# A four-layer graph network on one core: a third buffer for the radial weights, and one landing wait per block of gathers

## The reference

```python
# layer one: tensor product with per-edge weights from a small net
w  = silu(edge_attr @ w1 + b1) @ w2 + b2          # [E, 1024], "radial weights"
x0, x1 = x[src][:, :16], x[src][:, 16:].reshape(-1, 16, 3)
out0 = alpha * (einsum('eu,e,euw->ew', x0, sh0, w00) + einsum('eui,ei,euw->ew', x1, sh1, w11) / sqrt(3))
out1 = alpha * (einsum('eu,ei,euw->ewi', x0, sh1, w01) + einsum('eui,e,euw->ewi', x1, sh0, w10)) / sqrt(3)
...
# layer two: relations as sums of 8 bases; per-edge coefficients w_comp[edge_type]
# z[node, basis, :] = sum over its edges of coef[e, basis] * x[src[e]]
# layer three: graph convolution, a sum over the edges of scaled rows h[src[e]]
```

## Time and profile before

| | |
|---|---|
| median of 3 runs | 23,192.35 us |
| lowest and highest | 23,182.5 and 23,208.56 us |
| the profiled execution | 23,174.65 us |
| its span in the profile | 23,172.8 us |
| mean granted TensorE clock | 0.627 of full |

### The profile page before, as it was taken

One profiled execution on the slowest core, in us unless ns is written; L12 is line 12 of the kernel. 1 busy time (PEld: TensorE's weight loads), 2 busy tenths in 40 slices (PEclk: granted clock), 3 DMA queues, 4 the chain that ended last, 5 costly groups with the idle time before them and its releaser, 6 DMA issues. The chain is left out here.

```text
span 23172.8 us, 208220 instructions
## 1 busy us (share of the span) xinstructions
PE 10208.4 (44%) x47565; PEld 6761.2 (29%) x47566; DVE 15518.0 (67%) x25810; ACT 2702.6 (12%) x6634; POOL 12776.2 (55%) x12678
## 2 busy tenths in 40 slices
PE   0033335655555555555666632222234434344333
PEld 0033332222222222222222332222233333233333
DVE  8744447998888888887666521111477777677777
ACT  0011110000000000000000000000122332223322
POOL 0188886666565656644666426665355554455553
PEclk9999996555555555557888755555555555555555
DMA  4033331111111111111111101111422222222222
GB/s 176 21 69 69 70 69 28 24 24 24 23 22 23 22 24 21 24 22 22 24 24 24 17 13 21 21 21 20 59 61 61 56 58 51 58 63 60 57 59 47
DMA packets 1151509, 957.47 MB, mean 41 GB/s; under 512 B 803963, under 2 KB 920315, under 8 KB 1150739
## 3 DMA queue, kind: packets, MB, share of 16 engines
q0 software_dynamic: 419904, 437.84, 11.0%
q1 hardware_dynamic: 730960, 512.22, 8.6%
HBM read 734.68 MB, written 210.63 MB: 41 GB/s over the span
## 5 line engine op out<-in xcount | busy, mean ns | idle before, releaser
L1458 POOL DMA_INDIRECT tail<-ball,h_idx x3328 | 3445.4, 1035 | 3295.5 <-issue 1379.1
L737 PE MATMUL p_rad<-w_stack,hid_t 99*128 99x512 bf16 (+1 forms) x6656 | 3073.8, 619 | 2355.2 <-DVEq L827 1082.5
L1494 PE MATMUL h_sum<-head,h_hot 128*128 128x64 f32 x6656 | 1446.7, 417 | 3475.0 <-ACT head L1539 2117.5
L809 DVE TENSOR_REDUCE red<-prod 128x96 f32<-128x1536 f32 x1664 | 2900.2, 1743 | 3.5
L1494 PEld LDWEIGHTS h_sum<-head,h_hot 128*128 128x128 f32 x6656 | 1414.0, 327 | 3500.3 <-issue 3500.3
L1101 POOL DMA_INDIRECT l_xg<-h_tab,l_idx x1664 | 1573.9, 946 | 1462.7 <-issue 957.6
L338 POOL DMA_INDIRECT rec_a<-rec,slot x1600 | 1988.9, 1243 | 517.0 <-issue 501.4
L693 POOL DMA_INDIRECT rec_b<-l_rcb x1600 | 1929.8, 1206 | 570.9 <-issue 514.6
L932 POOL DMA_INDIRECT l_xg<-x_tab,l_idx x1664 | 1574.2, 946 | 1154.2 <-issue 834.1
L948 PE MATMUL l_sum<-outer,l_hot 128*128 128x512 f32 x3328 | 1684.6, 670 | 971.1 <-DVEq L993 899.5
L737 PEld LDWEIGHTS p_rad<-w_stack,hid_t 99*128 99x128 bf16 (+1 forms) x6656 | 773.3, 132 | 4300.7 <-issue 4298.8
(11 more groups left out here) (368 smaller groups left out, 18411.8 us busy)
## 6 DMA issues: line engine op xcount, KB each, us to landing
hot_t<-rows_l SPq DMA_DIRECT2D x208, 512.0 KB
rec_a<-fill SPq DMA_DIRECT2D x128, 728.0 KB, 19.6
l_rec<-rec_a SPq DMA_DIRECT2D x104, 896.0 KB, 4.8
rhot_t<-rows_r SPq DMA_DIRECT2D x208, 384.0 KB
tail<-ball,h_idx POOLq DMA_INDIRECT x3328
t<-in_type SPq DMA_DIRECT2D x100, 500.0 KB
l_xg<-in_x,l_idx POOLq DMA_INDIRECT x1664
l_xg<-x_tab,l_idx POOLq DMA_INDIRECT x1664
```

The source lines that it names most:

```text
L737: ins = pe.matmul(p_rad[j % 2][:, h * 512:(h + 1) * 512], hid_t[j // 4 % 2][0:K3 + 3 * (1 - i), j % 4, i, :], w_stack[i][0:K3 + 3 * (1 - i ...
L809: ch.step(dve.tensor_reduce(red[:, j, :], prod[j % 3][:, :, :], AX, ALU.add))
L1458: pool.indirect_dma_start(tg[q][:, j, :], None, table[:, :], bass.IndirectOffsetOnAxis(ap=idx[q][:, j:j + 1], axis=0)).then_inc(gathered[q ...
L1494: ins = pe.matmul(p_sum[u % 2][:, j % BT // 2, :], hot[j // HP8 % 2][:, j % HP8, :], hg[:, j, 0:D], start=(j % 2 == 0), stop=(j % 2 == 1))
```

## The change

In layer one the radial weights get a third buffer of two PSUM banks. PE takes tile j into buffer j % 3, makes three tiles of the next block before the sums of this one, and its waits for `tile_done` are renumbered: the first tile of a block waits for the last of the block before. In layers two and three POOL waits for landings once per block, after the sixteenth gather, and the index copies go from DVE to ACT. In layer two ACT makes them for block b+2 when block b-2 is used up, ahead of the coefficient copy of block b on its queue; in layer three for block b+4 when block b is summed.

```diff
@@ product_phase
-        p_rad = [ps(f"p_rad{q}", [P, COLS]) for q in range(2)]
+        p_rad = [ps(f"p_rad{q}", [P, COLS]) for q in range(3)]
...
             def tile(b, j):
-                hold(pe, turn, tile_done, b * BT + (j + 1))
+                hold(pe, turn, tile_done, b * BT + (3 if j == 0 else j if j < 3 else j + 1))
...
-                        ins = pe.matmul(p_rad[j % 2][:, h * 512:(h + 1) * 512], hid_t[j // 4 % 2][0:K3 + 3 * (1 - i), j % 4, i, :],
+                        ins = pe.matmul(p_rad[j % 3][:, h * 512:(h + 1) * 512], hid_t[j // 4 % 2][0:K3 + 3 * (1 - i), j % 4, i, :],
...
                 tile(b, 1)
+                tile(b, 2)
 
             def body(b, q, it, left):
-                for j in range(2, BT):
+                for j in range(3, BT):
...
-            dve.sem_inc(tile_done, SEED)
+            dve.sem_inc(tile_done, 3)
...
-                w = p_rad[j % 2][:, :].rearrange("p (a w u) -> p a w u", a=4, u=MUL)
+                w = p_rad[j % 3][:, :].rearrange("p (a w u) -> p a w u", a=4, u=MUL)
@@ relation_phase
-            with act.Fori(0, NB // 4) as it:
+            def indices(u, b):
+                act.activation(idx[u][:, :], g["src_a"][:, bass.ds(b * BT, BT)], ACT.Copy).then_inc(idx_ready, 1)
+
+            def quad(it, last):
                 for u in range(4):
                     b = it * 4 + u
+                    hold(act, turn, coef_used, b + 1)
+                    if not last or u < 2:
+                        indices((u + 2) % 4, b + 2)
                     hold(act, turn, coef_in[u], it * 32 + 32)
-                    hold(act, turn, coef_used, b + 1)
                     act.activation(p_coef[u % 2][:, 0:BT * NBAS].rearrange("p (t n) -> p t n", n=NBAS), coef[u][:, :, :], ACT.Copy).then_inc(coef_ready, 1)
+
+            for u in range(2):
+                indices(u, u)
+            with act.Fori(0, NB // 4 - 1) as it:
+                quad(it, False)
+            quad(NB // 4 - 1, True)
...
-                        if j % 8 == 7:
-                            hold(pool, turn, gathered[u], it * (16 * BT) + 16 * (j + 1))
+                    hold(pool, turn, gathered[u], it * (16 * BT) + 16 * BT)
...
-            for u in range(4):
-                dve.tensor_copy(idx[u][:, :], g["src_a"][:, u * BT:(u + 1) * BT]).then_inc(idx_ready, 1)
...
-                if left == 2:
-                    dve.tensor_copy(idx[u][:, :], g["src_a"][:, bass.ds((b + 4) * BT, BT)]).then_inc(idx_ready, 1)
@@ spread_phase: the same two edits to the gathers and to DVE, and on ACT
+            for u in range(4):
+                act.activation(idx[u][:, :], g["src_a"][:, u * BT:(u + 1) * BT], ACT.Copy).then_inc(idx_ready, 1)
+            with act.Fori(0, NB // 4 - 1) as it:
+                for u in range(4):
+                    b = it * 4 + u
+                    hold(act, turn, sum_done, b + 1)
+                    act.activation(idx[u][:, :], g["src_a"][:, bass.ds((b + 4) * BT, BT)], ACT.Copy).then_inc(idx_ready, 1)
```

## The result

The kernel before took 23,200.46 us (four runs beside the changed one, 23,182.5 to 23,209.55), the changed one 22,838.07 us (22,804.19 to 22,855.39). The ratio is 0.9843, 95% interval [0.9826, 0.986]: 362 us faster. The forecast was 22,290 us in a range up to 22,680; the time lies 158 us above the range. The sign and layer one were right, layer two went the other way.

What follows compares the result with a forecast made beforehand. DVE was taken to bound layer one, POOL's gathers and landing waits layers two and three. Savings of 385 + 260 + 257 = 902 us from 23,192 gave 22,290 us, range 22,190 to 22,680.

Steps and rivals of the forecast that it cites:

- Layer one, 385 us: Saving claimed for layer one from the third radial buffer: 153 + 312 - 80 us, with bounds of 153 and 465.
- third-tile term: Layer one: the third buffer removes DVE's stall at each block's third tile, 1.5 us x 102 blocks = 153 us.
- term for the seventh tile: Layer one: of 312 us of DVE stall at the seventh tile, about 80 us remain with PE one tile further ahead.
- late completions: Layer one: during a long gather stream, the semaphore telling DVE of a finished tile arrives late, about 3.9 us a block.
- The landing wait, 2.50 and 2.47 us a block: Layers two and three: replacing one landing wait per block by a plain gap saves 260 and 257 us.
- The page's fit for one transfer: Layers two and three: alternative estimate, 0.83 us per landing wait, 172 us saved in both; set aside for the trace.
- It stays 1.4 us below the new round: Layer two: DVE's own round of 21.05 us stays under the new 22.44 us, so the saving is whole.
- The rival of late completions: Layer two: late completions appear there, a 4 us hold per block eats the 260 us; time 22,550 us, chance 0.25.
- The slower rival: Layer two: holds of 10.2 to 12 us per block make the whole change lose, up to 23,380 us; chance 0.05.
- Layer three "has 18 us of cover and would not care": Layer three: PE waits 18 us of each 25 for gathers, so late completions would not reduce the 257 us.
- Index copies at 0: Layers two and three: moving 104 index copies per layer to ACT costs nothing; uncovered it would be 31 us.
- Thirteen early blocks without the stall: Layer one, 4,000 to 4,800 us: same gather streams, no late completions seen; argument against their appearing in layer two.

Runs made afterwards that it cites:

- a1: The changed kernel unaltered, run again beside the kernel before on another chip of the first kind: 22,640.46 us, ratio 0.987.
- e2: The kernel before with only the change to layer two, on a chip of the first kind: 23,154.7 us, ratio 1.0106.
- e1: The kernel before with only the third radial buffer of layer one, on a chip of the second kind: 22,369.22 us, ratio 0.9957.
- i1: The changed kernel unaltered, on a chip of the second kind: 21,858.33 us, ratio 0.9732.
- f2: The changed kernel with a 1.45 us POOL memset after the eighth gather in layers two and three, second kind of chip: 22,156.27 us, ratio 0.986.
- e4: The changed kernel with the landing wait per eight gathers put back in layer two, second kind of chip: 22,116.44 us, ratio 0.984.
- f3: The changed kernel with a 0.45 us POOL memset after the eighth gather in layer two, second kind of chip: 21,952.28 us, ratio 0.9765.
- g4: The kernel before with a 1.45 us POOL memset after the eighth gather in layer one, first kind of chip: 22,925.06 us, ratio 0.9985.
- e3: The kernel before with only the change to layer three, on a chip of the second kind: 22,221.84 us, ratio 0.9889.

## Why the prediction was right or wrong, step by step

**Layer one, 385 us: 388 measured.** The third-tile term, 153 us, was 152.7 in idle time. The term for the seventh tile, 312 - 80, was too small: nothing of the stall was left at DVE ("remote" 279.1 us before, 2.2 after), so idle time fell by 457. What I had not counted brought the sum back: the message and one-hot operations, 86 us longer, the message's beside POOL's features. (457 - 86 = 371; products and reductions are another 16 us shorter in sum.) The total agrees because two misses cancel, and by luck of the chip: on the chip of a1 and e2, also of the first kind, layer one goes from 6,860 to 6,589, 271 us. On the second kind the stall is absent, and of the 153 us the stage gains 107 and 112 (e1, i1) and only 91, 58 and 49 (f2, e4, f3). The longer messages take a part of the rest; why these runs differ stays open.

**The late completions, read in layer one.** "While a long stream of gathers is in flight, the semaphore that tells DVE of a finished tile arrives late": the tie to the stream is shown by g4, which added a pause to it and nothing else. The reading missed that beside a stream PE itself can slow down: in layers two and three of the result, and already in the fourth layer before, single passes stand apart.

**The landing wait, 2.50 and 2.47 us a block: right as a price.** On the second kind layer three gains 257 us (257 forecast) and layer two 2,619 - 2,368 = 251 (260 forecast). The page's fit for one transfer (the Trainium skill, DMA: Bandwidth & Descriptors, anatomy of one DMA on the SWDGE path), with its 172 us for both layers, is ruled out as the price of this wait by these 508 us. For the transfer itself the trace agrees with it: in layer two before, the last packet ends 2.12 us after the start of its gather (median of 198). POOL goes on only 1.5 us after that, and it is this which the estimate lacked.

**The step that failed** is "It stays 1.4 us below the new round. [...] So both savings are whole." It took DVE's round of 21.05 us in layer two as a property of its instructions. On the first kind of chip it depends on POOL's stream: the round became 2,875/104 = 27.6 us, DVE the bound, and the saving of 260 us a loss of 258. Against i1's 2,368 us the crawl costs 507 us, 4.9 us a block.

**The rival of late completions** (0.25) had the disturbance and its place right and named its signs. Its size was taken from layer one, one hold of 4 us per block, which would just eat the gain; DVE meets PE eight times a block there, and lost 21.05 to 27.6, 6.6 us. The slower rival had supposed 10 to 12. Truth lay between two sizes of one mechanism, and so the time came out above the range: 22,290 + 260 + 258 = 22,808, with layer three's 82 us 22,890, against 22,838 (the fourth layer, 17 us shorter in the profile, and the spread of the runs lie in the rest).

**Layer three "has 18 us of cover and would not care"** was wrong by 82 us (257 forecast, 175 measured): the crawl turns 7 us of sums into up to 32 of waiting (14563.95 above), more than the cover, and then POOL waits for its indices.

**Index copies at 0** held: i1 shows no wait on them, and where POOL waits for them it is for DVE's `coef_used` ahead of the copy.

**Thirteen early blocks without the stall** The earlier trace rows were taken as evidence against the rival, and the trace of the kernel before says otherwise. The earlier trace rows asked for DVE's waits only. In the same 800 us ACT waits under "remote" in five cases (138.0 us), and on the second kind (e3) in none. One of them, behind the last of eight transposes:

```profile
4037.06 0.31 PE L729 MATMUL l_turn<-l_ident_b,l_rec 128*96 128x128 bf16 x1
...
4042.83 1.02 ACT L713 ACTIVATE hid_t<-l_turn 96x1024 bf16<-96x1024 bf16 x1 [29.23 <-remote]
```

The copy starts 5.5 us after the transposes are modelled to end; the next one, with no gather in flight, starts 0.3 us behind its own (4047.24). So the late completions were there from the start and fell on ACT, which had idle time to spare. The one argument against the rival was a question put to one engine.

What stays open: by what path a stream of gathers slows PE, why a landing wait after eight of them is enough in two layers and not in the fourth, and why it happens on three of six chips and the result's, and not on the other three. Granted clock (0.50 in layer three in both kinds; 0.81 and 0.85 in layer two), the cadence of the gathers (1.25 us in both) and the bytes moved (957.96 and 957.94 MB) don't tell the kinds apart.

## What to carry to other kernels

A wait that looks like pure loss may also be the pause that another engine lives on. Before a landing wait is taken out, look in the trace for any place where the stream already runs that long, and ask for the waits of every engine there, not only of the one that bounds the stage: an engine with idle time can be the one that shows the disturbance. A stall found in one stage gives no size for another: once per block was too little here (4 us), once for each of eight meetings with PE would have been far too much (32 us), and 6.6 us were measured. If a stall has no releaser in the profile, run the same kernel on another chip before building a term on it: here 312 us of one sum existed on one kind of chip only. And where the wait is to go, try a short pause of known length in its place: 1.45 us after the eighth gather gave back 354 and 361 us on two chips of one kind, and would cost 122 (2,490 against 2,368) on the other.

## What the runs showed of the hardware that was not expected

- Two kinds of chips: the same kernel takes 22,471 to 22,480 us on three and 22,857 to 23,200 elsewhere. Part of that lies where no edit was made: the fourth layer, which has a landing wait after each eighth gather, takes 6,248 to 6,271 us on the second kind and 6,471 to 6,641 on the first.
- Sixteen indirect gathers in a row, 1.25 us apart, slow PE on the first kind in layers two and three: passes of 0.27 us with 0.4 to 2.6 us between. In layer one they only delay the word of PE's finished work, by 5.5 us in the case shown. In the fourth layer eight in a row do it. Pauses of 0.45 and 1.45 us after the eighth cut layer two from 2,854 to 2,711 and 2,493 us.
- A DVE operation of 128x768 with both inputs in SBUF takes 0.95 us alone and 1.37 to 1.56 beside arithmetic of POOL (layer one of the result, 93 of 104 times). The product of the same size with one input in PSUM takes 0.95 us in both cases (170 of 1,664 times beside POOL in the kernel before).
